# Taking the short filler products out of a TensorE stream, in four places of a steady step

## The reference, cut to what matters

```python
for W, a_s, a_d, bg, R, g, b in layers:          # 3 graph layers on 50 joints of a pose
    h = _gat(x, src, dst, W, a_s, a_d, bg)       # attention over a joint's neighbours
    res = x @ R
    x = gelu(_layer_norm(h + res, g, b))
x = x.reshape(Bb * Tt, J * DIMS[-1]) @ fpW + fpb
x = _layer_norm(x, fng, fnb)                     # one 128-wide token for each pose
...
h = concatenate([tok(x), txt], axis=1)
h = h + attn(_layernorm(h))                      # projections, a causal convolution, a memory
h = h + ffn(_layernorm(h))                       # 8 experts of 128-512-128, the best 2 weighted
```

## Time and profile before

| | |
|---|---|
| median of 3 runs | 4794.21 us (4791.25 to 4811.75) |
| the profiled execution's own time | 4790.66 us |
| its span, first to last instruction | 4788.9 us |
| mean granted TensorE clock | 0.970 |
| PE busy | 4235.0 us (88%) |
| DVE busy | 3576.6 us (75%) |
| ACT busy | 2610.1 us (55%) |
| filler products (L612) in the whole execution | 388 |

### The profile page before, as it was taken

One profiled execution on the slowest core, in us unless ns is written; L12 is line 12 of the kernel. 1 busy time (PEld: TensorE's weight loads), 2 busy tenths in 40 slices (PEclk: granted clock), 3 DMA queues, 4 the chain that ended last, 5 costly groups with the idle time before them and its releaser, 6 DMA issues.

```text
span 4788.9 us, 62742 instructions
## 1 busy us (share of the span) xinstructions
PE 4235.0 (88%) x22774; PEld 1933.7 (40%) x22774; DVE 3576.6 (75%) x8027; ACT 2610.1 (55%) x3929; POOL 632.2 (13%) x746
## 2 busy tenths in 40 slices
PE   4688989899998988989998898989899898999988
PEld 4223343443434334343433434344343433434345
DVE  1677788777778877777787777788777887777772
ACT  0454656556565555656555565555556565565643
POOL 1110201111020111102011120111102011110100
PEclk9798999999999999999999999999999999999998
DMA  2000000000000000000000000000000000000000
GB/s 96 2 1 3 1 3 3 2 4 1 3 3 3 3 1 6 1 3 3 3 3 1 6 1 3 3 2 4 1 3 3 3 3 2 5 1 3 3 2 6
DMA packets 22964, 24.35 MB, mean 5 GB/s; under 512 B 3394, under 2 KB 21834, under 8 KB 22138
## 3 DMA queue, kind: packets, MB, share of 16 engines
q1 hardware_dynamic: 22650, 20.26, 1.4%
HBM read 16.06 MB, written 4.19 MB: 4 GB/s over the span
## 4 chain that ended last, share of the span: by engine, by line
PE 62%; DVE 22%; ACT 9%; issue 5%; POOL 1%; SPq 0%; DMA 0%; DVEq 0%; ACTq 0%; POOLq 0%
PE bank L859 11%; PE bank L812 7%; PE bank L925 7%; PE bank L916 6%; PE bank L696 4%; PE bank L829 3%; ACT X L1264 3%; PE bank L770 3%; PE bank L850 2%; PE bank L815 2%; DVE X L1870 2%; DVE Ho L2019 2%; PE bank L832 1%; PE bank L708 1%; PE bank L759 1%
## 5 line engine op out<-in xcount | busy, mean ns | idle before, releaser
L1870 DVE TENSOR_TENSOR X<-X,bank 128x1024 f32<-128x1024 f32 (+2 forms) x432 | 483.5, 1139 | 273.3 <-PE bank L736 152.1
L1264 ACT ACTIVATE X<-X,c_vec 128x1024 f32<-128x1024 f32 (+2 forms) x432 | 497.6, 1174 | 309.5 <-DVE X L1870 308.6
L1308 ACT ACTIVATE X<-bank,bgc 128x512 f32<-128x512 f32 (+1 forms) x624 | 418.6, 671 | 418.7 <-PE bank L859 416.8
L916 PE MATMUL bank<-XT,c_w 128*128 128x512 f32 x1024 | 500.1, 613 | 44.6 <-ACT SQ L1344 42.6
L925 PEld LDWEIGHTS bank<-c_w,SQ 128*128 128x128 f32 x4096 | 481.9, 192 | 56.5 <-issue 50.2
L925 PE MATMUL bank<-c_w,SQ 128*128 128x128 f32 x4096 | 500.8, 277 | 0.0
L532 POOL TENSOR_TENSOR R<-X 128x512 f32<-128x512 f32 (+1 forms) x208 | 257.2, 1240 | 1576.0 <-PE bank L812 796.4
L812 PE MATMUL bank<-R,c_W 64*128 64x512 f32 (+1 forms) x832 | 457.6, 630 | 7.6 <-ACT R L1292 2.9
L859 PE MATMUL bank<-R,c_C 128*128 128x512 f32 (+1 forms) x832 | 455.5, 629 | 0.0
L846 PE MATMUL bank<-X,WR 64*128 64x512 f32 (+1 forms) x832 | 448.8, 624 | 0.0
L1344 ACT ACTIVATE SQ<-bank,c_vec 128x512 f32<-128x512 f32 x512 | 344.8, 685 | 152.4 <-PE bank L916 143.3
(11 more groups left out here) (257 smaller groups left out, 6853.9 us busy)
## 6 DMA issues: line engine op xcount, KB each, us to landing
c_w<-in_w SPq DMA_DIRECT2D x2, 2048.0 KB
out<-Ho SPq DMA_DIRECT2D x32, 128.0 KB, 1.9
c_fpW<-in_fpW SPq DMA_DIRECT2D x1, 3200.0 KB
X<-in_x SPq DMA_DIRECT2D x34, 75.0 KB, 2.0
X<-in_txt SPq DMA_DIRECT2D x32, 64.0 KB, 1.8
X<-in_chain SPq DMA_DIRECT2D x1, 1300.0 KB
X<-in_sel SPq DMA_DIRECT2D x1, 600.0 KB
X<-in_sel SPq DMA_DIRECT2D x1, 300.0 KB
```

What stands on the lines that cost most here:

```text
L916: mm(hidden_bank(e, m), w1[:, k * P:k * P + P], XT2[:], start=True, stop=True).then_inc(hid_ps, 1)
L1264: A_(dst, dst, ACT.Gelu, bias=v(f"b{l}"), scale=v(f"g{l}")).then_inc(x_ok, 1)
L1308: A_(dst, bZ[k % 2][:, 0:cols], ACT.Identity, bias=bias).then_inc(zs_ok, 1)
L1870: TT(dst, dst, b, ALU.mult).then_inc(u_ok, 1)
```

## The change

In the steady steps the short groups of filler products are taken out: two ahead of each of the three inner `variance` calls of layer 0, four ahead of the last score product of layer 0's norm, two each at pairs 2 and 3 of layer 1's norm, two ahead of the transposes of layer 2's attention weights, and two and one at pairs 2 and 3 of layer 2's norm. The layer-0 groups stood only in windows with an expert block in flight (14 windows), those of the two other norms in all 16 steps, those ahead of the transposes in 15. The longer groups of 8, 12, 18 and 30 in the first two steps stay.

```diff
@@ window: layer 0
                         own_0(w, n)
                         if n % 4 == 1 and n >= 5:
-                            if moe:
-                                keep_warm(2, bank[0])
                             variance(w, 0, n // 4 - 1)
@@ window: norm of layer 0
                         down(t - 1, 5, (2, 3))
-                    if moe and m == PAIRS[0] + 1:
-                        keep_warm(4, bank[0])
                     if m < PAIRS[0]:
                         spread_rstd(w, 0, m)
@@ iteration: norm of layer 1
                         down(t, 0, (3,))
-                    if m in (2, 3):
-                        keep_warm(2, bank[4])
                     if m < PAIRS[1]:
@@ iteration: ahead of the transposes for layer 2
-                alpha_parts(s, 2, 2 if tail else 30)
+                alpha_parts(s, 2, 0 if tail else 30)
@@ iteration: norm of layer 2
                             down(t, 4, (3,))
-                        keep_warm(2, bank[4])
-                    if m == 3:
-                        keep_warm(1, bank[0])
                     if m < PAIRS[2]:
```

## The result

| | before | after |
|---|---|---|
| median | 4793.99 us (4 runs, 4791.25 to 4811.75) | 4866.83 us (4 runs, 4864.54 to 4869.30) |
| profiled span | 4788.9 us | 4866.7 us |
| mean granted clock | 0.970 | 0.937 |

The changed kernel is slower: ratio 1.0144, 95% interval 1.0119 to 1.0169, some 73 us. (The ratios here are those on record; they can differ from the quotient of two printed medians by 0.1%.) That is outside the stated range (4779 to 4848), beyond rival 2 (4851), to which 0.22 was given.

The account below looks back on a forecast made before the run. It took TensorE, busy 88% and 62% of the chain, to bound the kernel, with the clock's falls priced too. 4790.7 - 13.5 + 24 + 3.5 = 4805 us profiled, about 4809 as median; range 4779 to 4848.

Parts of the forecast that it names:

- rival 2: Layer 0, L708 to L723: clock low throughout, 5 us a step, 70 us less 13.5 of gains, 4851 us; chance 0.22.
- What bounds the kernel, and the price of the clock: Whole kernel: TensorE busy 88%, 62% of the chain; each us at 1.2 GHz costs 0.34 to 0.41 us.
- Waits behind the fillers: Layer 2's transposes gain 0.43 us x 15 = 6.5 us; norms of layers 1 and 2 and layer 0's variances gain 0.
- A new spell in layer 0: Around the last variance group: a new stretch at 1.2 GHz in nearly all 14 steps, 24 us lost, bounds 0 and 53.
- the term after it: Start of layer 0: an existing low-clock stretch may last longer in five steps; 7 us at half odds, 3.5 us lost.
- I count no new spell there: Norms and ahead of transposes: TensorE stays densely busy, no new low-clock stretch, loss 0, bounds 0 to 20 us.
- the 13.5 us booked as gains: 6.5 us ahead of layer 2's transposes plus 7 at the end of layer 0's norm; bounds 0 and 16.
- The gain of 7 us at the end of layer 0's norm: Four fillers removed inside low-clock stretches whose end TensorE doesn't shift; 7 us taken, between 0 and 9.5.
- Two counts: Of 14 windows, 13 have a low-clock stretch at the end of layer 0's norm, five one at layer 0's start.
- Rival 1: Layer 0: the clock doesn't fall, only the gains of 13.5 us stay, 4781 us; chance 0.20.
- the page's rule of idle gaps: Skill page advises only against gaps over about 3 us; largest here grows to 1.7, so removal would cost nothing.
- Rival 3: Faster: more removed products on the path, or displaced steps lose the long norm-end low-clock stretch; 4748 us together, chance 0.08.

Follow-up runs that it names:

- e9: e8 with seven more fillers a step at the start of layer 1 and one at the start of layer 0: 4741.11 us, ratio 0.9921.
- e15: e9 without the two fillers ahead of layer 2's transposes: 4743.85 us, ratio 0.9918.
- e13: e9 without the fillers in the norms of layers 1 and 2, ahead of layer 2's transposes and at the end of layer 0's norm: 4741.85 us.
- e7: Kernel before, with the fillers of layer 0's variances on 32 instead of 120 array rows, same number, place and columns: 4825.69 us, ratio 1.0096.
- e14: e9 without the filler groups of layer 0's variances, its one at n == 4 kept: 4773.87 us, ratio 0.9979.
- e2: The changed kernel with the three groups ahead of layer 0's variance sums put back, the other 198 fillers out: 4843.30 us, ratio 1.0118 to before.
- e4: Kernel before without the fillers of the norms of layers 1 and 2 and the two ahead of layer 2's transposes: 4817.81 us, ratio 1.0061.
- e5: Kernel before without the two fillers ahead of layer 2's transposes: 4808.31 us, ratio 1.0060.
- e6: Kernel before with four instead of two fillers ahead of layer 2's transposes, nothing removed: 4823.46 us, ratio 1.0092.
- e1: Kernel before without the three groups of two fillers ahead of layer 0's variance sums (84 products), all others kept: 4881.99 us, ratio 1.0201.
- e3: Kernel before without the four fillers ahead of the last score product of layer 0's norm (56 products): 4836.92 us, ratio 1.0101.
- e12: Kernel before with 16 instead of 8 fillers once, in the very first window, steady steps untouched: 4778.94 us, ratio 0.9996.
- e8: Kernel before with more fillers where TensorE idles: layer 0's variances, last pairs of its norm, end of layer 1's norm: 4770.84 us, ratio 0.9971.

## Why the prediction was wrong, point by point

- **What bounds the kernel, and the price of the clock**: right. 0.34 to 0.41 us a us was read from two differences between steps; over 221 steps it is 0.30.
- **Waits behind the fillers**: right. In clean steps the transposes gained their 0.43 us and the norms nothing (279.6 us in e9, about 279.15 in e15 and also in e13, where the norms' fillers are out too). In layer 0's variances TensorE's wait grew by what was removed.
- **A new spell in layer 0**: it came in every steady step, as said, and e7 and e14 show that the missing work lets the clock fall there. With the other idle places filled it costs 33 us (e14 against e9, where 14 fillers a step are out instead of six), where the sum had 24, within the bounds of 0 to 53.
- **The first step that failed, and the largest, is the size of that spell in the changed kernel**: "I take 1.7 us: 14 x 1.7 = 24 us lost", worked out for one short spell that begins around the last variance group, some 12 us into the layer, with the waits for L723 as cover. In the trace the clock falls 3 to 5 us into the layer and is low for 17 to 24 us in each step, and the stretch from L708 to L723 is 4.8 us a step longer than before. Over 14 steps that is some 67 us, against 24 and the 3.5 of the term after it, and beyond the bound of 53. Rival 2 described that case, its condition (over 7 us low in layer 0) and its 5 us a step.
- **The second step that failed** is "in the norms and ahead of the transposes ... I count no new spell there", together with the 13.5 us booked as gains. With layer 0's groups in, the deletions in these places alone lose 56 us (e2). Most of it isn't a fall where the products were missing: of the 16.0 us at the lower clock that e2 adds to a step, 9.4 lie in layer 0, whose fillers it has. e4 and e5 also have more of it there, and e6 the same with work added. In the kernel before the steps happened to pass most idle places (layer 0, the end of its norm, 75, 150 and 180 us behind layer 0's start) without a fall, 9.2 us a step against 14.7 to 32.8 in every variant that changed only its short groups. The prediction named this ("where the falls land once the steps have another length") as unsure and gave it no term. How much of the 67 us in layer 0 comes from the fillers missing there and how much from such displacement can't be split: the stretch to L723 is 3.9 us longer in e1 and 2.9 in e2.
- **The gain of 7 us at the end of layer 0's norm** rested on "the spell ends at a time that TensorE doesn't shift". Where the spell was 10.2 us in both, the gain is there: from L754's start to the memory block's first product 10.93 us before (1576.63 to 1587.56) and 10.37 after (1892.88 to 1903.25). But a spell of 3.4 us became one of 6.8 without the four fillers (e3), and time at the lower clock at this place went from 6.0 to 10.8 us a step, so on the whole it was no gain.
- **Two counts** of the prediction are off: in the trace of before, 12 of the 14 windows have a spell at the end of the norm, not 13, and 7 have one at the start of layer 0, not five. Neither moves the sum by more than 2 us.
- **Rival 1 and the page's rule of idle gaps**: not borne out. The idle times in layer 0's variances were about 1.8 us, once 1.9, and the clock fell in each step. The Trainium skill, "TensorE: Matmul & The Clock Gate", section "Why this matters for your kernels", warns only of much longer gaps; the measurement decides.
- **Rival 3** named the displacement too, but with the sign of a gain. Nothing in the rows spoke for either sign. That the kernel before was a lucky case, so that most displacements would lose, became plain only from the experiments.

What stays open: why just the lengths near that of the kernel before meet few spells, and why e3 loses 50 us though its clean steps should be no shorter (e13 and e15 have clean steps of the same length, with and without the four out); that its longer spell at the norm's end displaces the next step is likely, not shown. e5, e6 and e12 show that 0.43 us a step matters and a single shift of 1.7 to 3.5 us does not; no run maps the dependence.

## What to carry to other kernels

Price the clock before the products: a filler that stands in another engine's wait costs nothing (clean steps of 279.6 us with and without e8's), and taking it out can cost several us a step (e1), because the clock can fall in that wait. A loop whose steps repeat and have several half-idle places reacts to a small edit by more than the edit, whichever way the edit goes (e5 and e6). Fill the idle places first (e9: steps of 279.6 us at 1.00): small edits then move the time by 3 us or less (e13 and e15 against e9), though still not by what their waits say, since a few short spells eat a gain of 6.5 us. When two halves of a change lose more apart than together, look for a shared state such as the clock and not for a third cost.

## What the runs showed of the hardware

- Two fillers more in each step, 0.43 us of work, made the kernel 0.9% slower (e6), two fewer 0.6% (e5).
- Products of the same columns on 32 instead of 120 rows didn't keep the clock up in layer 0: spells of 6.8 to 13.7 us in every steady step (e7), against 1.6 us a step on average before, in spells of 3.4.
- Four fillers of 0.22 us each at full clock decided whether a spell at the end of layer 0's norm lasted 3.4 or 6.8 us, with the same busy time ahead of it (e3 against before).
- A us at 1.2 GHz costs this kernel 0.30 us on average, not one half; that waits for other engines cover the rest is the likely reason, not shown by itself.
